# A pre-norm attention and channel-mix block on one Trainium2 core: pair sums of the last group moved to VectorE, and four seams between the stages rearranged

## The chip, the core and the metric

The kernel runs on one core of one Trainium2 chip. Its time is that of the whole program on the device, in microseconds, as a median over runs. Five engines work side by side, each through its own queue of instructions, in order: TensorE (PE, with its weight loads as PEld), VectorE (DVE), ScalarE (ACT), GpSimd (POOL) and SyncE (SP), which only issues transfers here. They meet through semaphores.

## What is computed

Cut to what matters, for `x` of shape (8, 1024, 512) in fp32:

```
x = x + attn(layernorm(x));   x = x + mix(layernorm(x))

attn(x): ct_q = x Wdq + b;  q = heads(ct_q Wuq + b) + heads(rope(ct_q Wqr + b))
         ct_kv = x Wdkv + b; k = heads(ct_kv Wuk + b) + heads(rope(x Wkr + b)); v = heads(ct_kv Wuv + b)
         softmax(q k^T / scale) v  (16 heads of 32)  -> Wo + b
mix(x):  x_prev = x shifted by one token
         xr = mu_r x + (1 - mu_r) x_prev;  xk = mu_k x + (1 - mu_k) x_prev
         sigmoid(xr Wr^T) * (relu(xk Wk^T)^2 Wv^T)
```

## The kernel before

All products are taken with operands split into a high part in the format of TensorE's fast fp32 and a low remainder, as high*high + high*low + low*high, so each product has three matmuls for each 128 of depth. Work goes through four stages, each a block that ends when all engines have ended it: `fold_block` (weights multiplied together), `project_block`, `attend_block`, `mix_block`.

**Projection.** 16 chunks of 512 tokens (two per batch). In each, eight items give q and k, four give v; the high and low parts go through a ring of four buffers to memory. In the last chunk TensorE also computes, between the items, the score products of which the row maxima of the first attention group are taken (`max_product`, with VectorE's `max_reduce`); these maxima are needed before the exponentials.

**Attention.** 32 groups, each of four heads of one batch, in three slots (`load_group` brings q, k and v of a group by ten loads on SP's queue). A group has two halves of queries; a half has four units, a unit eight score products `scores` of 128 keys x 512 queries (L977). ScalarE takes each to its exponential (L1097), `pv` multiplies them with the values (L990), and GpSimd adds the two halves of a unit's exponentials pairwise (L1124), joins the four pair sums to two (one by an accumulating transfer, L1128, and one by an addition, L1131), whose column sums TensorE takes in `sums` (L1004). ScalarE may be three units ahead of pair sums and values. Between its scores TensorE computes the maxima products of the next group (L413), in the order `USE`: 32 tiles of half 0, two of half 1, the transpose of half 0's row maxima (L408), 30 tiles, the transpose of half 1. VectorE reduces each (L429) and writes the negated maxima (L426); SP copies them under the q stack (`stack_max`). How many maxima stand before each score is the table `SPREAD`: one before each of the eight, a second one at the third score of unit 4 (this is where the transpose of half 0 comes to lie), and one behind the value unit of unit 7. The first group has a table of its own, since its next group is loaded only at the start of this stage: none in its first two units, eleven in each of the others. Slot 1 lies in memory that only this stage owns; slots 0 and 2 are overlaid with buffers of other stages.

In the last group there are no more maxima. Meanwhile VectorE inverts the softmax sums of seven batches (L1148), multiplies the heads of the mix's first chunk with them (L1151), and takes the low parts of two weights and of that chunk. ScalarE makes their high parts (L1071, L1094), between units. GpSimd adds the pairs of all units but the last.

**Mix.** 16 chunks again. TensorE's order in chunk c is: output projection of chunk c+1 (`project`), key product (out of `xk`), receptance product (`xr`), transposes of the normalised chunk c+1, value product; 48 matmuls each but for the transposes. The others' work runs a chunk ahead. VectorE: residual of chunk c+1 (L1509; TensorE's key product waits for it tile by tile, since it reuses its banks), statistics, normalise (L1525), four low parts of the squared relu (L1594, `square_lo`), the shift (difference L1537, mix L1540 and L1548, with the four gatings L1603 between), and low parts of it (L1583, L1585). GpSimd: power for the deviation, four squares (L1469), the product of the heads of chunk c+2 with the inverse sums (L1442, `divide`), their low part (L1446, `o_low`), the final additions and bias additions in turn (L1482, L1451). ScalarE: relu, high parts, sigmoid. The prologue of this stage prepares chunks 0 and 1; the shift of its chunk 0 is done by quarters of the features (`first_shift`), all others whole.

## Time and profile before

| | |
|---|---|
| median of 3 runs | 3108.95 us (3105.3 to 3110.42) |
| profiled execution, its own time | 3107.7 us |
| its span | 3105.7 us |
| mean granted TensorE clock | 0.987 |
| TensorE busy | 3013.7 us, 97% of the span |
| VectorE, ScalarE, GpSimd busy | 2249.6 us, 1487.7 us, 2095.4 us |
| attention, from its first score product | from 661.54 us |
| mix, from its first transfer | from 2309.01 us |

Spans are measured from the first instruction; the profiled execution's own time has some 2 us around it. Busy times of TensorE are modelled, so a full slice isn't yet TensorE at its peak. The idle time of an engine that is not the bound costs nothing.

### The profile page before, as it was taken

To read this page: it belongs to the slowest core of one execution; us is meant where nothing else is said; L and a number is where in the kernel's file an instruction comes from. 1 tells how busy PE (TensorE), PEld (TensorE's weight loads), DVE (VectorE), ACT (ScalarE), POOL (GpSimd) and SP (SyncE) were. 2 spreads that over 40 slices of the span, in tenths; PEclk is the share of its full clock that TensorE was granted. 3 is DMA by queue.
4 is the path that set the end of the run, shared out by engine and by line. 5 is a ranking of instruction groups with operands and counts; after the bars stand their busy time and mean duration, and the time that the engine had idled before them with its cause. 6 is when DMAs were issued, how large, how long until landed. Compare 5 with 4: busy or idle time off the path is not lost. (4 is left out here: it accounts for less than half of the span.)

```text
span 3105.7 us, 42723 instructions
## 1 busy us (share of the span) xinstructions
PE 3013.7 (97%) x15424; PEld 2007.0 (65%) x15424; DVE 2249.6 (72%) x3352; ACT 1487.7 (48%) x2715; POOL 2095.4 (67%) x715
## 2 busy tenths in 40 slices
PE   8999999989999999999999999999987999999998
PEld 5888888855555555555555555555536787878776
DVE  5555665568777777777777777777748777777784
ACT  2222222126666666666666666666652323223222
POOL 1111121128999999999999999999974665665663
PEclk9999999989999999999999999999988999999999
DMA  4554545664646464656555565646351323323311
GB/s 147 173 173 166 177 163 174 184 158 105 138 109 147 100 147 104 146 110 137 120 127 128 121 134 122 136 111 146 86 144 41 109 74 88 108 61 101 108 54 41
DMA packets 189193, 381.77 MB, mean 123 GB/s; under 512 B 17360, under 2 KB 53360, under 8 KB 180976
## 3 DMA queue, kind: packets, MB, share of 16 engines
q1 hardware_dynamic: 179968, 313.70, 36.8%
q0 software_dynamic: 9072, 66.06, 10.4%
q8 instruction: 92, 1.51, 0.2%
q14 instruction: 61, 0.50, 0.1%
HBM read 194.59 MB, written 118.49 MB: 101 GB/s over the span
## 5 line engine op out<-in xcount | busy, mean ns | idle before, releaser
L429 DVE TENSOR_REDUCE part_max<-ps_m 128x1 f32<-128x512 f32 x1984 | 1214.4, 682 | 333.6 <-PE ps_m L413 332.8
L1124 POOL TENSOR_TENSOR pairs<-probs 128x2048 f32<-128x2048 f32 x255 | 1187.3, 4662 | 144.8 <-ACT probs L1097 133.7
L1097 ACT ACTIVATE probs<-ps_s 128x512 f32<-128x512 f32 x2048 | 1037.0, 623 | 290.9 <-PE ps_s L977 275.1
L413 PE MATMUL ps_m<-k_stack,q_stack 96*128 96x512 f32 x1984 | 820.8, 415 | 15.7 <-DVE neg_max L426 8.5
L977 PE MATMUL ps_s<-q_stack,k_stack 97*128 97x512 f32 x2048 | 818.0, 403 | 6.9 <-PEq L461 3.7
L413 PEld LDWEIGHTS ps_m<-k_stack,q_stack 96*128 96x128 f32 x1984 | 376.6, 190 | 286.9 <-DVE part_max L429 136.8
L990 PE MATMUL ps_o<-probs,v_tiles 128*32 128x512 f32 x4096 | 498.4, 605 | 0.0
L977 PEld LDWEIGHTS ps_s<-q_stack,k_stack 97*128 97x128 f32 x2048 | 389.4, 191 | 135.7 <-ACT probs L1097 21.5
L676 POOL TENSOR_TENSOR ln_rstd<-ln_rstd,ln_minus_half 128x4 f32<-128x4 f32 x15 | 15.1, 1008 | 413.5 <-DVE ln_rstd L718 413.5
L1131 POOL TENSOR_TENSOR pairs<-pairs 128x2048 f32<-128x2048 f32 x63 | 288.6, 4581 | 4.9
L990 PEld LDWEIGHTS ps_o<-probs,v_tiles 128*32 128x32 f32 x4096 | 107.6, 109 | 235.5 <-issue 177.2
L1482 POOL TENSOR_TENSOR gate<-gate,xs 128x512 f32<-128x512 f32 x64 | 115.3, 1804 | 131.7 <-DVE diff L1548 114.3
L1403 ACT ACTIVATE relu<-mix_p 128x512 f32<-128x512 f32 x64 | 38.3, 598 | 239.8 <-PE mix_p L1288 188.4
L1594 DVE TENSOR_TENSOR ka_lo<-relu,ka_hi 128x512 fp32r<-128x512 f32 x64 | 109.3, 1707 | 50.4 <-ACT ka_hi L1397 48.2
L1067 ACT COPY l_sb<-ps_s 128x512 f32<-128x512 f32 x64 | 37.5, 586 | 175.7 <-PE ps_s L1004 174.6
L1004 PE MATMUL ps_s<-pairs,ones 128*32 128x512 f32 x1008 | 119.7, 592 | 0.0
L1286 PE MATMUL mix_p<-xk_hi,mix_w_k_hi 128*128 128x512 f32 x256 | 103.7, 405 | 13.1 <-DVE xs L1509 9.0
L1451 POOL TENSOR_TENSOR xs<-mix_x_in,bo 128x512 f32<-128x512 f32 x64 | 113.2, 1773 | 4.5
L761 DVE TENSOR_TENSOR st_v<-ps_p,bv 128x512 f32<-128x512 f32 x64 | 44.2, 691 | 99.3 <-PE ps_p L595 99.3
L1469 POOL TENSOR_TENSOR relu<-relu 128x512 f32<-128x512 f32 x64 | 68.8, 1084 | 66.7 <-ACT relu L1403 66.7
L1286 PE MATMUL mix_p<-mix_w_v_hi,ka_hi 128*128 128x512 f32 x256 | 102.6, 401 | 11.3 <-DVE ka_lo L1594 11.3
L563 PE MATMUL ps_p<-xT_hi,w_q_hi 128*128 128x512 f32 x256 | 102.1, 399 | 1.5 <-DVE y_rot L783 1.5
(196 smaller groups left out, 4804.7 us busy)
## 6 DMA issues: line engine op xcount, KB each, us to landing
pairs<-pairs POOLq DMA_DIRECT2D x63, 1024.0 KB, 8.0
q_stack<-q_hi_scratch SPq DMA_DIRECT2D x128, 256.0 KB, 6.2
k_stack<-k_hi_scratch SPq DMA_DIRECT2D x64, 512.0 KB, 10.9
x_in<-in_x SPq DMA_DIRECT2D x16, 1024.0 KB, 5.6
q_hi_scratch<-st_hi SPq DMA_DIRECT2D x64, 256.0 KB, 2.2
q_lo_scratch<-st_lo SPq DMA_DIRECT2D x64, 256.0 KB, 2.5
k_hi_scratch<-st_hi SPq DMA_DIRECT2D x64, 256.0 KB, 2.4
k_lo_scratch<-st_lo SPq DMA_DIRECT2D x64, 256.0 KB, 2.6
```

Of the source, the lines that this page charges most:

```text
L413: nc.tensor.matmul(bank[:, :], att["q"][r][0:ROWS, half, h, q * P:(q + 1) * P], att["k"][r][0:ROWS, h, kc * CH:(kc + 1) * CH], start=True, ...
L429: nc.vector.reduce_max(part_max[:, half, j, kc:kc + 1], bank[:, :], AX).then_inc(att["m_read"], 1)
L977: nc.tensor.matmul(ps_s[v % SR][:, :], ks[r][:, a, kt * P:(kt + 1) * P], qs[r][:, qc, a, :], start=True, stop=True).then_inc(scored, 1)
L990: m = nc.tensor.matmul(ps_o[a * HD:(a + 1) * HD, :], vt[r][:, kt, a * HD:(a + 1) * HD], probs[:, (r * UNITS + u) % PR, k, a, :], start=kt ...
L1004: m = nc.tensor.matmul(ps_s[v % SR][a * HD:(a + 1) * HD, :], ones[:, :], pairs[:, w, a, :], start=k == 0, stop=k == SUMS - 1)
L1097: nc.scalar.activation(probs[:, (r * UNITS + u) % PR, x // HG, x % HG, :], ps_s[place(u * UT + x) % SR][:, :], ACT.Exp, scale=SCALE).then_ ...
L1124: nc.gpsimd.tensor_tensor(pairs[:, w, :, :], probs[:, (r * UNITS + u) % PR, 0, :, :], probs[:, (r * UNITS + u) % PR, 1, :, :], ALU.add).th ...
L1131: nc.gpsimd.tensor_tensor(pairs[:, 3, :, :], pairs[:, 2, :, :], pairs[:, 3, :, :], ALU.add).then_inc(pair_done, 1)
L1286: nc.tensor.matmul(out, stat_hi(f), mov_hi(f), start=f == 0, stop=False)
L1451: nc.gpsimd.tensor_tensor(xs[par][:, s, :], x_in[:, s, :], bo[:, :], ALU.add).then_inc(xb_done, 1)
L1482: nc.gpsimd.tensor_tensor(gate[s], gate[s], xs[par][:, s, :], ALU.add).then_inc(out_done, 1)
L1594: nc.vector.tensor_tensor(ka_lo[:, g, :], relu[:, g % RELU, :], ka_hi[:, g, :], ALU.subtract).then_inc(kal_done, 1)
```

## The change

1. `USE` puts the transpose of half 0 behind eight tiles of half 1 instead of two, and `SPREAD` sets it behind the value unit of unit 4.
2. The load of group 1 moves from the start of the attention into SP's queue ahead of the stores of the last projection chunk. Its slot now lies over the room of the projection's `x_in`, on the right side of the memory. SP's waits for the stacked maxima (dropped) and for the value stores (moved into the attention stage) no longer stand at the projection's end. The first group uses `SPREAD` like all others.
3. In the last group GpSimd does nothing. VectorE adds seven pairs and both joins, and makes the three high parts that were ScalarE's; the first join is an addition instead of a transfer.
4. In the mix prologue VectorE takes residual and statistics of chunk 0 first, then the product of heads of chunk 1 (GpSimd's before), the normalise, the low part of those heads (GpSimd's before), a weight, the shift by quarters, the residual of chunk 1, and only then the inverse of the last batch's sums and the low part of `xr`.
5. In every `divide` of the mix loop GpSimd first waits for the four low parts of the squared relu.
6. The shift for the last chunk is done by quarters too, and its four output tiles are stored one by one.

```diff
-USE = tiles(0, 0, HALF_TILES) + tiles(1, 0, 1) + [(0, HALF_TILES, 0)] + tiles(1, 1, HALF_TILES) + [(1, HALF_TILES, 0)]
+UNIT_TILES = HALF_TILES // 4
+USE = (tiles(0, 0, HALF_TILES) + tiles(1, 0, UNIT_TILES) + [(0, HALF_TILES, 0)]
+       + tiles(1, UNIT_TILES, HALF_TILES) + [(1, HALF_TILES, 0)])
...
+                    if last and par == CPB - 1:
+                        sp.wait_ge(transposed, B * CPB * FC)
+                        load_group(sp, att, grouped, 1, 1)
...
-            for half in range(2):
-                sp.wait_ge(att["m_stacked"][half], 16)
...
-            load_group(sp, att, scratch, 1, 1)
+            for s in att["v_stored"]:
+                sp.wait_ge(s, 16 * B * CPB)
...
-        SPREAD[ROUNDS][2] = 2
+        SPREAD[ROUNDS][UT] = 1
         SPREAD[UNITS - 1][UT] = 1
-        SPREAD_FIRST = [[0] * (UT + 1) if u < 2 else [2, 1, 1, 2, 1, 1, 2, 1, 0] for u in range(UNITS)]
...
+                pair(0)
+                pair(1)
+                pair_onto(1, n * NQ, joined_last)
+                pair(2)
+                dve.wait_ge(mix["inv_stored"], 16)
+                weight_high("o")
+                pair(3)
+                pair_onto(3, n * NQ, pair_done)
+                weight_low("o", 1)
+                pair(4)
+                weight_high("k")
                 dve.wait_ge(mix["o_loaded"], 16)
                 dve.wait_ge(mix["inv_loaded"], 16 * HG)
                 nc.vector.tensor_tensor(mix["o_in"][:], mix["o_in"][:], mix["o_lo"].bitcast(F32), ALU.mult).then_inc(mix["o_div"], 1)
-                weight_low("o", 1)
+                pair(5)
                 weight_low("k", 2)
+                dve.wait_ge(mix["o_div"], 1)
+                nc.vector.tensor_copy(mix["o_hi"], mix["o_in"][:]).then_inc(mix["oh_done"], 1)
+                pair(6)
...
                     if two_more:
+                        pool.wait_ge(kal_done, c * FC + FC)
                         divide(c + 2)
...
             weights_low(2)
+            residual(0, 0)
+            statistics(0, 0)
+            dve.wait_ge(o_loaded, 32)
+            dve.wait_ge(inv_loaded, 32 * HG)
+            nc.vector.tensor_tensor(o_in[:], o_in[:], first_inverse[:].bitcast(F32), ALU.mult).then_inc(o_div, 1)
+            normalise(0, 0)
+            dve.wait_ge(oh_done, 2)
+            nc.vector.tensor_tensor(o_lo[:], o_in[:], o_hi[:], ALU.subtract).then_inc(ol_done, 1)
+            weights_low(3)
+            dve.wait_ge(small_loaded, 16 * 3)
+            quarter_shift(0, 0, 0)
+            residual(1, 1)
             dve.wait_ge(l_loaded, 32)
             nc.vector.reciprocal(inv, sums).then_inc(inv_done, 1)
-            dve.wait_ge(small_loaded, 16 * 3)
-            norm(0, 0)
-            weights_low(3)
-            first_shift()
-            first_shift_low()
+            shift_low_r(0)
...
-                    if more:
+                    if last and par == CPB - 2:
+                        quarter_shift(c + 1, 1 - par, FC - 1, gated_value)
+                        shift_low_r(c + 1)
+                    elif more:
                         shift(c + 1, 1 - par, i if par == 0 else i + 1, gated_value)
...
+                    if last and par == CPB - 1:
+                        for s in range(TPC):
+                            sp.wait_ge(out_done, c * TPC + s + 1)
+                            sp.dma_start(out_v[i, par, :, s, :], gate[s]).then_inc(out_stored, 16)
+                        return
```

`pair(u)` is the addition of L1124 on VectorE with the same waits, `pair_onto(w, ...)` the join of two pair sums. `quarter_shift` is the former `first_shift`, with the chunk's gatings between its quarters.

## Rows read from the trace of the kernel before

**Rows 1.** Busy time by engine, steady attention: PE, PEld, DVE, ACT, POOL, clock, DMA.
```profile
760.00:2196.00 1436.00, 1428.28 (x8230) 790.16 (x8230) 1132.25 (x1929) 982.84 (x1929) 1350.15 (x342) 1.00 0.56 125
```

**Rows 2.** Timeline of VectorE, second and last transpose of half 1 (start, us, instruction).
```profile
727.54 0.28 DVE L426 TENSOR_SCALAR neg_max<-ps_m 16x128 fp32r<-16x128 f32 x1 [0.45 <-PE ps_m L408]
...
2246.52 0.28 DVE L426 TENSOR_SCALAR neg_max<-ps_m 16x128 fp32r<-16x128 f32 x1 [0.45 <-PE ps_m L408]
```

**Rows 3.** Timeline of VectorE and GpSimd, mix; eleven chunk distances between the first and last difference.
```profile
2529.03 2.29 DVE L1537 TENSOR_TENSOR diff<-xT 128x2048 f32<-128x2048 f32 x1
...
2570.01 1.96 DVE L1594 TENSOR_TENSOR ka_lo<-relu,ka_hi 128x512 fp32r<-128x512 f32 x2 [1.23 <-ACT ka_hi L1397]
2572.47 4.61 POOL L1442 TENSOR_TENSOR o_in<-o_in,o_lo 128x2048 f32<-128x2048 f32 x1 [1.88 <-DMA o_lo<-inv_scratch]
2576.31 2.91 DVE L1537 TENSOR_TENSOR diff<-xT 128x2048 f32<-128x2048 f32 x1 [4.34 <-ACT xT L1368]
...
3048.52 2.29 DVE L1537 TENSOR_TENSOR diff<-xT 128x2048 f32<-128x2048 f32 x1 [4.35 <-ACT xT L1368]
```

**Rows 4.** Timeline of TensorE, start of the attention.
```profile
661.54 8.17 PE L977 MATMUL ps_s<-q_stack,k_stack 97*128 97x512 f32 x16 [3.72 <-PEq L461]
...
679.60 0.77 PE L413 MATMUL ps_m<-k_stack,q_stack 96*128 96x512 f32 x1 [6.72 <-DMA k_stack<-k_lo_scratch]
```

**Rows 5.** Timeline of ScalarE, last group.
```profile
2266.44 1.90 ACT L1071 CAST mix_w_o_hi<-raw_o 128x2048 fp32r<-128x2048 f32 x1 [2.73 <-DMA inv_scratch<-early_inverse]
...
2275.97 4.03 ACT L1097 ACTIVATE probs<-ps_s 128x512 f32<-128x512 f32 x8 [1.92 <-PE ps_s L977]
...
2281.49 4.03 ACT L1097 ACTIVATE probs<-ps_s 128x512 f32<-128x512 f32 x8
```

**Rows 6.** Timeline of VectorE and TensorE, last group.
```profile
2277.26 6.50 DVE L1151 TENSOR_TENSOR o_in<-o_in,o_lo 128x2048 f32<-128x2048 f32 x1 [24.80 <-DMA o_lo<-inv_scratch]
...
2305.14 1.89 PE L1019 MATMUL ps_s<-probs,ones 128*32 128x512 f32 x16
```

**Rows 7.** Timeline of VectorE and TensorE, mix prologue.
```profile
2324.41 0.95 DVE L1614 RECIPROCAL gate<-gate 128x128 f32<-128x128 f32 x1 [10.47 <-DMA gate<-l_scratch]
...
2331.95 6.09 DVE L1525 TENSOR_SCALAR mixed<-xs,mix_mv,mix_rstd 128x512 f32<-128x512 f32 x4 [1.15 <-POOL mix_rstd L1435]
...
2338.10 3.58 PE L1309 MATMUL mix_t<-ident,mixed 128*128 128x128 f32 x16 [17.76 <-DVE mixed L1525]
...
2357.41 2.29 DVE L1579 TENSOR_TENSOR xr_lo<-diff,xr_hi 128x2048 fp32r<-128x2048 f32 x1 [1.96 <-ACT xr_hi L1376]
...
2360.45 0.76 PE L1286 MATMUL mix_p<-xk_hi,mix_w_k_hi 128*128 128x512 f32 x1 [7.84 <-DVE xs L1509]
```

**Rows 8.** Timeline of TensorE, first key product of the last chunk.
```profile
3062.89 0.80 PE L1286 MATMUL mix_p<-xk_hi,mix_w_k_hi 128*128 128x512 f32 x1 [4.03 <-DVE xk_lo L1583]
```

**Rows 9.** Timeline of TensorE, starts of units in one steady group, and a value unit.
```profile
1511.84 0.50 PE L413 MATMUL ps_m<-k_stack,q_stack 96*128 96x512 f32 x1
...
1518.29 0.50 PE L413 MATMUL ps_m<-k_stack,q_stack 96*128 96x512 f32 x1
...
1522.22 1.92 PE L990 MATMUL ps_o<-probs,v_tiles 128*32 128x512 f32 x16
...
1537.41 0.28 PE L408 MATMUL ps_m<-ident,row_max 128*16 128x128 f32 x1
...
1543.39 0.50 PE L413 MATMUL ps_m<-k_stack,q_stack 96*128 96x512 f32 x1
```

**Rows 10.** Groups by line: the normalise (count, total us, mean ns).
```profile
L1525 DVE TENSOR_SCALAR mixed<-xs,mix_mv,mix_rstd 128x512 f32<-128x512 f32 x64 | 55.7, 929 | 18.1 <-POOL mix_rstd L1435 18.1
```

**Rows 11.** Busy time by engine in the last group; PEclk is the seventh number.
```profile
2272.00:2276.00 4.00, 4.00 (x18) 1.17 (x11) 0.00 (x0) 2.08 (x3) 3.59 (x1) 0.50 0.97 201
```

**Rows 12.** Waits: us in total, times, longest us.
```profile
PE mix_p L1286 <- DVE ka_lo L1594: 11.3, 11, 1.5
```

**Rows 13.** Transfers: count, KB each, median us to landing.
```profile
out<-gate SPq DMA_DIRECT2D x16, 256.0 KB, 3.8
```

More of the change, by code:

```diff
@@ L497, in project_block @@
         stored = [sem(f"stored{i}") for i in range(RING)]
-        v_stored = [sem(f"v_stored{i}") for i in range(TPC)]
+        v_stored = att["v_stored"]
         block = ctx.enter_context(nc.Block())
@@ L1067, in take_l @@
                 nc.scalar.copy(l_sb[:, qc, :], ps_s[v % SR][:, :]).then_inc(exped, 1)
-            def weight_high(k):
-                act.wait_ge(mix["w_loaded"][k], 16)
-                nc.scalar.copy(mix["w_hi"][k], mix["w_raw"][k]).then_inc(mix["w_split_hi"], 1)
             def step(i, r, n):
@@ L1125, in step @@
                                             ALU.add).then_inc(pair_done, 1)
-                    if w == 1 and not at_the_end:
+                    if w == 1:
                         pool.wait_ge(pair_done, h * ADDS + 2)
@@ L1141, in weight_low, with pair, pair_onto @@
                     nc.vector.tensor_tensor(mix["w_lo"][k], mix["w_raw"][k], mix["w_hi"][k], ALU.subtract).then_inc(mix["w_split_lo"], 1)
+                def pair(u):
+                    qc, w = divmod(u, ROUNDS)
+                    h = n * NQ + qc
+                    if w == 0 and qc == 0:
+                        dve.wait_ge(joined, 16 * h)
+                        dve.wait_ge(pair_done, h * ADDS)
+                    elif w == 0:
+                        dve.wait_ge(joined_last, 1)
+                    elif w == 1:
+                        dve.wait_ge(sum_done, (h - 1) * SUMS + 1)
+                    elif w == 3:
+                        dve.wait_ge(sum_done, h * SUMS)
+                    dve.wait_ge(exped, taken(n, place(u * UT + UT - 1)))
+                    nc.vector.tensor_tensor(pairs[:, w, :, :], probs[:, (r * UNITS + u) % PR, 0, :, :], probs[:, (r * UNITS + u) % PR, 1, :, :],
+                                            ALU.add).then_inc(pair_done, 1)
+                def pair_onto(w, h, done):
+                    dve.wait_ge(pair_done, h * ADDS + w + 1)
+                    nc.vector.tensor_tensor(pairs[:, w, :, :], pairs[:, w - 1, :, :], pairs[:, w, :, :], ALU.add).then_inc(done, 1)
                 if not is_last(n):
@@ L1488, in _ @@
                 add_bias(0, 0, s)
-            divide(1)
             inv_std(0)
-            o_low(1)
             edge(0)
@@ L1527, in norm @@
                 v.then_inc(normed, 1)
+            def norm(c, par):
+                if not (type(c) is int and c == 1):
+                    residual(c, par)
+                statistics(c, par)
+                normalise(c, par)
             def shift(c, par, batch, free_bank=lambda s: None):
@@ L1645, in block_program, with overlaid @@
         t = {"ident": lasting("ident", [P, P])}
-        def overlaid(buffers, *which):
+        def overlaid(buffers, *which, side="left"):
             with ExitStack() as passing:
-                return buffers(lambda name, shape, dt=F32: passing.enter_context(nc.sbuf_tensor(name, shape, dt)), *which)
+                return buffers(lambda name, shape, dt=F32: passing.enter_context(nc.sbuf_tensor(name, shape, dt, side=side)), *which)
         slot0 = overlaid(slot_buffers, 0)
@@ L1663, in block_program @@
             "loaded": [sem(f"stack_loaded{r}") for r in range(R3)],
+            "v_stored": [sem(f"v_stored{i}") for i in range(TPC)],
             "v_loaded": [sem(f"vt_loaded{r}") for r in range(R3)],
@@ L1683, in block_program @@
                  for k in ("q_hi", "q_lo", "k_hi", "k_lo", "v_hi", "v_lo", "rot")}
-            x_in = [sb(f"x_in{i}", [P, TPC, D]) for i in range(CPB)]
+            x_in = [early.enter_context(nc.sbuf_tensor(f"x_in{i}", [P, TPC, D], F32, side="right")) for i in range(CPB)]
+            early.enter_context(nc.sbuf_tensor("slot1_rest", [P, SLOT - CPB * TPC * D], F32, side="right"))
             x_loaded = [sem(f"x_loaded{i}") for i in range(CPB)]
```

112 lines of the change are left out of this document (61 added, 51 removed).

## The prediction

> **What bounds the kernel now.** I read the page first (shares, slices, chain), then windows by stage, then the timeline of each engine around each edit. In the attention stage TensorE is the bound: over 1436 us it is busy 1428.28 us at full clock, GpSimd 1350.15, VectorE 1132.25 [rows 1]. So there only TensorE's own stretches count, as long as GpSimd, at 94%, keeps its small slack. Group to group takes (2246.52 - 727.54) / 30 = 50.63 us [rows 2]. In the mix TensorE is nearly the bound, but a ring through VectorE and GpSimd comes out slightly longer than its work: the difference of one chunk follows that of the chunk before after (3048.52 - 2529.03) / 11 = 47.23 us [rows 3]. At the seams TensorE stands still: before the first group and inside it [rows 4], behind late exponentials in the last group [rows 5, 6], 17.76 and 7.84 us in the mix prologue [rows 7], and 4.03 us before the last chunk [rows 8]. The change touches all of these.
>
> **T behind a value unit (30 groups).** Unit 4 now holds the transpose of half 0 in its middle and lasts 1518.29 - 1511.84 = 6.45 us. The transpose of half 1 is already behind a value unit, with the same queue after it, and that unit of eight scores, eight maxima and one value unit lasts 1543.39 - 1537.41 = 5.98 us, transpose included [rows 9]. The new place of half 0 is the same situation, with the same bank two tiles on and its row maxima long done. So 0.47 us a group, 30 groups: **-14.1**. Bounds: -9, if one third of it is lost to GpSimd, whose slack of (1436 - 1350) / 1436 x 50.63 = 3.0 us a group is well over 0.47; -15.5 if nothing at all is left of a wait. The stacking of half 0's maxima starts some 5 us later and is needed twenty us on; hidden.
>
> **Group 1 loaded early; the first group like the others.** Before, TensorE starts the attention at 661.54 after 3.72 us, runs two units without maxima, waits 6.72 us for the k stack of group 1, and reaches the transpose of half 1 at about 727.5: 66.0 us [rows 2, 4]. After, the ten loads of group 1 stand in the last projection chunk, and SP waits neither for the maxima's row nor for the value stores before the block ends. The first group is then a steady one, 50.63 - 0.47, less a value unit and a pair of sums that a first group hasn't (16 records, 1.92 us in the row, about 1.8 each) = 46.5 us. TensorE has stood still before it and its clock is then at 1.2 GHz: the matmul at 679.60 takes 0.77 us where one behind a value unit took 0.50 [rows 4, 9]; I add 3 us for that, as much as some 15 matmuls at 0.43 instead of 0.23. 66.0 - 49.5 = -16.5, and about -1.2 for SP's shorter wait: **-17.7**. Bounds: -21 without the clock's loss, -11 if twice that and the loads' cost come. The loads: SP issues them ahead of all stores of the last projection chunk, where it otherwise waits for the first low half, and its queue is shared by both. VectorE sets the pace of that chunk and gets its input from a ring of four, so a store may be late by three items without harm. If the cover were gone, the whole transfer would show, which the 6.72 us of [rows 4] size; it is the lower bound above. The copies of the row of ones and the load of group 2 follow as before, with half the traffic beside them.
>
> **Last group.** Its eight pair sums, each 4.6 us on GpSimd, and both joins go to VectorE, the DMA join becomes an addition, and ScalarE loses three copies. Price on VectorE: 128x2048 with two SBUF inputs took 2.29 us with GpSimd idle [rows 3]; 7 pairs + 2 joins + 4 mix operations = 13 x 2.3, three copies of 2.3 each (no row shows a VectorE copy; it lies between nothing and 4 x 0.93 = 3.7, what four normalises of together as many elements took [rows 10]; I take 2.3, the two-input price, as the nearest in shape), and the reciprocal, about 5: 42 us in a group of over 50, and 46 at the upper price. VectorE therefore keeps up, unless it waits: its product of heads waits for the inverse, which landed at 2277.26 [rows 6], and pair 5, weight k and everything behind it are queued there; pair 4 is ahead of it and its exponentials end near then, so nothing waits. The gain is what ScalarE waited: it stood 2.73 us for the stored inverse and copied 1.90 us, then 1.89 us for weight k, where the plain distance of units is 2281.49 - 2275.97 = 5.52 us [rows 5]. Laid out anew: 0.4 + 8 x 5.52 + 2 sums of 1.8 + 2.8 (three pair sums) + 1.8 + 1.8 = 54.6 us after 2246.52, that is 2301.1, against 2305.14 + 1.89 = 2307.03 [rows 6]: -5.9. But TensorE's clock was at 1.2 GHz from 2272 to 2276 [rows 11], after units in which ScalarE's pace left it waiting; that will recur in part. **-5**, bounds -8 and 0.
>
> **Mix prologue.** Before, VectorE idles 10.47 us for the last group's sums, in the queue behind a weight and four inverses, and only then takes the residuals, though TensorE had finished them at 2338.10 - 17.76 = 2320.34. From 2324.41 to the normalise at 2331.95 are 7.54 us, of which 0.95 the reciprocal and 2.4 four residuals; 4.2 stay. New: 2320.34 + 0.7 + 4.2 + 2.3 (product of heads, now VectorE's) = 2327.5, and four normalises not held by GpSimd's o_low: 4 x 0.93 = 3.7 at most instead of 6.09 [rows 7, 10]; transposes at 2331 instead of 2338.10. From there to the first key product, 2360.45, were 22.4 us. Added o_low 2.3; gone from that path are the wait of 1.96 and the 2.29 of xr_low, since the residual of chunk 1 stands ahead of them: 20.4. 2351.1 against 2360.45: **-9.3**. GpSimd's bias additions still fall on the quarter shift, as before. What is put off: the last inverse is stored some 5 us into the first key product, so ScalarE's first relu is about 1 us late and SP's loads for chunk 2 are behind it; the product that needs these has over 10 us. Bounds -12 and -5.
>
> **GpSimd's product waits for all four ka_low (14 chunks).** This is the place where a rule and the wish part. Before, the product is issued ahead of the last ka_low, which then takes until its end, and TensorE waits 11.3 / 11 = 1.0 us for it [rows 12]. Twice the inverse was late, so that the trace shows what the edit will do every time: the two last ka_low took 1.96 us together, the product started 1.88 us late and ended at 2577.08, and now the next difference met it and took 2.91 instead of 2.29 us [rows 3]. From difference to last ka_low in that chunk: 2571.97 - 2529.03 = 42.94 us; plus 0.1 and 4.6 for the product, less 0.15 (2.91 - 2.29 against 0.77 of overlap): the ring is 47.4 to 47.5 us, against 47.23. So the wait moves from TensorE's value product to its key product, behind a residual: **+2.6** for 13 distances. Bounds: -9, TensorE's own 46.5 us; +5, if 0.15 isn't given back and an inverse is late.
> The Trainium skill, page "SBUF — State Buffer", section "Who interferes with whom", says that a VectorE operation with two SBUF inputs and a GpSimd one that reads SBUF exclude each other for a whole instruction, whoever comes first. By that rule the collision is only handed on, as the row has it (the sum +2.6); without it the sum would be the -9 above.
>
> **Last chunk by quarters, and its stores.** TensorE waits 4.03 us for xk_low and goes on at 1.2 GHz: its first matmul takes 0.80 us where one after a short wait took 0.50 [rows 8, 9]; about twelve at 0.43 for 0.23 lose 2.4. By quarters VectorE can start with the first transposed quarter, some 1.4 us ahead of the 3048.52 of [rows 3], and needs four differences, four mixes and four lows of 0.6 to 0.8 us each and three gates between, 15 x 0.68 = 10.2 us: xk_low is done at about 3057.3, ahead of the value product's end at 3062.89 - 4.03 = 3058.9: **-6.4**, bounds -7.5 and -3. The last store is 256 KB alone; behind 768 KB it took 3.8 us to land [rows 13], of which its own share by size is a quarter and a fixed part isn't known: **-1.3**, between 0 and -2.8.
>
> **Sum.** -14.1 - 17.7 - 5 - 9.3 + 2.6 - 6.4 - 1.3 = -51.2, from the profiled execution's own 3107.7 us (span 3105.7): 3056.5. That execution lies 1.25 us under the median 3108.95; so **3057** as a median.
>
> **Rivals.**
> A: the ring is not what holds the mix, and the wait on ka_low frees TensorE: 46.5 us a chunk instead of 47.4. Sum -9 in place of +2.6: 3046. For it: TensorE waited for ka_lo at 11 places, 11.3 us in all [rows 12]. Against it: the two late products [rows 3].
> B: the moved transpose gives nothing, because GpSimd at 94% or the banks take it back: -37, 3071. Against it: the twin at half 1 [rows 9].
> C: the early load disturbs the last projection chunk, or the first group runs long at 1.2 GHz: about 12 us less, 3069. For it: the slow start of [rows 4, 11].
> D, slower than before: the later product makes o_low late. Product, ScalarE's copy and o_low are a line; if o_low then lost the port to the whole shift, it would end some 9 us after TensorE wants to project, 14 times 9 = 126 us: 3057 + 126 = 3183. Counted from the end of the transposes, the product ends at 1.9, copy and o_low take 1.9 + 4.6 and up to 0.4 behind the difference, 8.8; the value product's 48 matmuls last 11. So the slack is 2.2 us, and the sum turns round from 2.2 + 51 / 14 = 5.8 us of lateness. Against it: the product comes only 1 us later, and in the late chunks the ring hardly grew [rows 3].
>
> **Chances and range.** Forecast 0.65, A 0.13, B 0.08, C 0.10, D 0.04. The forecast's own range, its bounds combined as independent, is 3047 to 3067; A and C stretch it: **3043 to 3071**. What can be told from no change here is 0.2%, 6 us. Faster 0.95, same 0.01, slower 0.04.
>
> **What will show it.** Transposes of half 0 followed by no wait, groups of 50.2 us. No long wait for k_stack, the first group under 52 us. No GpSimd work in the last group, and its units 5.5 us apart. First key product about 41 us after the first projection. ka_low never above 1.2 us, but differences of 2.9 us and waits of key products for the residual; a chunk of 47.4 us. No wait before the last key product. I am wrong if a group is still 50.6, if the mix's chunk is under 47, or if the exponentials of the last group wait for VectorE's pairs.

## The result and the profile after

The changed kernel takes 3060.54 us as a median of four runs, against 3108.43 of the kernel before beside it: a ratio of 0.9848, 95% interval 0.9831 to 0.9865. The forecast was 3057, range 3043 to 3071. The profiled execution took 3059.14 us itself, its span is 3057.4 (before 3107.7 and 3105.7), so the traces differ by 48.3 us of span. One execution of a kernel below (the product by quarters with spread matmuls) took 14671.14 us and is left out of its median. The rows that answer to those of before follow, stage by stage.

Timeline of VectorE: the transposes of half 1 that answer to [rows 2]; between them lie 30 groups.
```profile
708.94 0.28 DVE L429 TENSOR_SCALAR neg_max<-ps_m 16x128 fp32r<-16x128 f32 x1 [0.49 <-PE ps_m L411]
...
2215.86 0.28 DVE L429 TENSOR_SCALAR neg_max<-ps_m 16x128 fp32r<-16x128 f32 x1 [0.49 <-PE ps_m L411]
```
The first came 18.6 us earlier, and the group is (2215.86 - 708.94) / 30 = 50.23 us, 0.40 less.

Timeline of TensorE: the start of the attention ([rows 4]) and, in a later group, unit 4 with the transpose of half 0 ahead of it, and the sums behind it ([rows 9]).
```profile
660.10 0.77 PE L416 MATMUL ps_m<-k_stack,q_stack 96*128 96x512 f32 x1 [2.03 <-PEq L464]
...
1487.17 0.50 PE L416 MATMUL ps_m<-k_stack,q_stack 96*128 96x512 f32 x1
...
1491.12 1.92 PE L991 MATMUL ps_o<-probs,v_tiles 128*32 128x512 f32 x16
1492.98 0.28 PE L411 MATMUL ps_m<-ident,row_max 128*16 128x128 f32 x1
1493.01 0.48 PE L416 MATMUL ps_m<-k_stack,q_stack 96*128 96x512 f32 x1
1493.63 0.50 PE L416 MATMUL ps_m<-k_stack,q_stack 96*128 96x512 f32 x1
...
1498.85 1.90 PE L1007 MATMUL ps_s<-pairs,ones 128*32 128x512 f32 x16
```
The maxima start in the first unit, and the wait of 6.72 us for the k stack is gone; from the first matmul to the transpose of half 1 are 48.8 us instead of 66.0. The plain unit lasts 1492.98 - 1487.17 = 5.81 us, the next one, transpose included, 1498.85 - 1492.98 = 5.87.

Timeline of TensorE in the last group, and two 4 us stretches of it by engine (PEclk is the seventh number), for [rows 6, 11].
```profile
2219.25 1.92 PE L991 MATMUL ps_o<-probs,v_tiles 128*32 128x512 f32 x16
...
2224.96 3.35 PE L991 MATMUL ps_o<-probs,v_tiles 128*32 128x512 f32 x16
...
2244.64 3.39 PE L991 MATMUL ps_o<-probs,v_tiles 128*32 128x512 f32 x16
...
2251.80 3.58 PE L991 MATMUL ps_o<-probs,v_tiles 128*32 128x512 f32 x16
...
2272.23 1.90 PE L1022 MATMUL ps_s<-probs,ones 128*32 128x512 f32 x16
```
```profile
2224.00:2228.00 4.00, 4.00 (x18) 1.01 (x22) 2.29 (x1) 1.75 (x4) 0.00 (x0) 0.57 1.04 399
2244.00:2248.00 4.00, 4.00 (x19) 0.81 (x18) 4.00 (x3) 1.64 (x4) 0.00 (x0) 0.62 0.00 0
```
Three of the group's eight value units (from 2224.96 on) run at half clock, between 1.92 us ones. GpSimd is idle, as meant, and TensorE ends at 2274.13, 58.3 us after the transpose of half 1; before it was 60.5.

Timeline of TensorE in the prologue: first projection, transposes, first key product, for [rows 7].
```profile
2276.31 0.47 PE L1318 MATMUL mix_p<-mix_w_o_hi,o_hi 128*128 128x512 f32 x1 [2.18 <-PEq L854]
2296.45 3.46 PE L1341 MATMUL mix_t<-ident,mixed 128*128 128x128 f32 x16 [9.01 <-DVE mixed L1568]
2316.58 0.77 PE L1318 MATMUL mix_p<-xk_hi,mix_w_k_hi 128*128 128x512 f32 x1 [5.73 <-DVE xs L1546]
```
The 17.76 us of waiting are 9.01, the 7.84 are 5.73; from first projection to first key product 40.27 us, before 2360.45 - 2309.21 = 51.24.

Timelines of VectorE and GpSimd in the mix, for [rows 3]: the first difference, one chunk, and the fourteenth difference.
```profile
2343.26 2.29 DVE L1586 TENSOR_TENSOR diff<-xT 128x2048 f32<-128x2048 f32 x1 [8.28 <-ACT xT L1400]
...
2574.41 1.96 DVE L1651 TENSOR_TENSOR ka_lo<-relu,ka_hi 128x512 fp32r<-128x512 f32 x2 [1.23 <-ACT ka_hi L1433]
2580.01 3.35 DVE L1586 TENSOR_TENSOR diff<-xT 128x2048 f32<-128x2048 f32 x1 [3.64 <-ACT xT L1400]
...
2961.44 3.38 DVE L1586 TENSOR_TENSOR diff<-xT 128x2048 f32<-128x2048 f32 x1 [3.60 <-ACT xT L1400]
```
```profile
2576.61 4.60 POOL L1480 TENSOR_TENSOR o_in<-o_in,o_lo 128x2048 f32<-128x2048 f32 x1 [1.62 <-DVE ka_lo L1651]
```
The waits of TensorE, in total us, times, longest, for [rows 12]:
```profile
PE mix_p L1318 <- DVE xs L1546: 21.3, 14, 5.7
```
The ka_low are undisturbed. The product starts 0.24 us behind the last of them and ends at 2581.21, 1.20 us after the difference was issued, which therefore takes 3.35 instead of 2.29. TensorE's wait for ka_low has become one for the residual ahead of the key product. Thirteen distances are 618.18 us. Before, the same two differences stood at 2387.79 and 3001.24, 613.45 us apart: this stage costs 4.7 us. One of the thirteen is 48.37 us long: there the inverse landed late, and the product stood 0.91 us behind the last ka_low. Some 0.8 of the 4.7 is that.

In the last chunk there is no wait for xk_low. Timeline of SyncE's queue and GpSimd: the last two stores, which one row holds, and GpSimd's last addition:
```profile
3052.13 3.10 SPq L1304 DMA_DIRECT2D out<-gate  x2
3053.62 1.26 POOL L1521 TENSOR_TENSOR gate<-gate,xs 128x512 f32<-128x512 f32 x1 [1.51 <-DVE gate L1660]
```

| term | forecast | trace |
|---|---|---|
| T behind a value unit, 30 groups | -14.1 | -12.1 |
| early load, first group | -17.7 | -18.6 |
| last group, to the first projection | -5 | -2.2 |
| prologue (forecast to the first key product, trace to the first difference of the loop) | -9.3 | -11.6 |
| product waits for ka_low, 13 distances | +2.6 | +4.7 |
| last chunk, 14th difference to last gate product | -6.4 | -6.6 |
| stores | -1.3 | -1.9 |
| sum | -51.2 | -48.3 |

### The profile page after: what moved, and what is told of

Same layout as the page of the kernel before. It is cut to its first block and busy times, and to the rows that moved or that the text cites. A ratio compares the mean times of both kernels' runs of the same rounds, so it can differ in the third digit from the quotient of the medians.

```text
span 3057.4 us, 42730 instructions
## 1 busy us (share of the span) xinstructions
PE 2998.4 (98%) x15424; PEld 2002.8 (66%) x15424; DVE 2216.4 (72%) x3372; ACT 1480.5 (48%) x2715; POOL 2041.7 (67%) x704
## 5 line engine op out<-in xcount | busy, mean ns | idle before, releaser
L1113 POOL TENSOR_TENSOR pairs<-probs 128x2048 f32<-128x2048 f32 x248 | 1155.6, 4672 | 110.2 <-ACT probs L1087 110.1
L1546 DVE TENSOR_TENSOR xs<-mix_p,xs 128x512 f32<-128x512 f32 x64 | 43.8, 688 | 85.7 <-POOL xs L1489 81.2
L1318 PE MATMUL mix_p<-mix_w_o_hi,o_hi 128*128 128x512 f32 x256 | 100.1, 391 | 2.4 <-PEq L854 2.2
```

The lines of the kernel that those rows point to most:

```text
L1113: nc.gpsimd.tensor_tensor(pairs[:, w, :, :], probs[:, (r * UNITS + u) % PR, 0, :, :], probs[:, (r * UNITS + u) % PR, 1, :, :], ALU.add).th ...
L1318: nc.tensor.matmul(out, stat_hi(f), mov_hi(f), start=f == 0, stop=False)
```

## The experiments

Every time is a median beside runs of the kernel before on the same chip; the intervals of the ratios are 0.0013 to 0.0017 to either side, 4 to 5 us. So sizes below that are read from the stages of the traces, each of one execution. "The changed kernel" is the one of the diff.

### The wait on ka_low: taken away, and loosened by one

```diff
-                        pool.wait_ge(kal_done, c * FC + FC)
                         divide(c + 2)
```


> The changed kernel, but GpSimd's product of heads no longer waits for the four ka_low. Theory (the wait only hands the collision on, and costs a little): the mix's distance from difference to difference falls from 47.65 us back to about 47.2, the differences (3.3 us in the changed kernel) take 2.3 again, the last ka_low reach past 2 us, and TensorE waits about 1 us a chunk for ka_low instead of for the residual; 13 x 0.43 = 5.6 us less than the changed kernel's 3060.5: about 3055. Rival A of the prediction (the wait frees TensorE): without it the distance grows, 3070 or more.

Measured: 3052.66 us, ratio 0.9825 (0.9811 to 0.9838). Thirteen distances are 613.74 us, 47.21 each; the difference is 2.29 (2.93 once, behind a late inverse), TensorE waits 11.2 us for ka_low in 12 places. Timelines of one chunk, VectorE and GpSimd:
```profile
2667.28 6.14 DVE L1650 TENSOR_TENSOR ka_lo<-relu,ka_hi 128x512 fp32r<-128x512 f32 x2 [1.23 <-ACT ka_hi L1433]
2673.76 2.29 DVE L1585 TENSOR_TENSOR diff<-xT 128x2048 f32<-128x2048 f32 x1 [0.34 <-ACT xT L1400]
```
```profile
2667.82 5.05 POOL L1480 TENSOR_TENSOR o_in<-o_in,o_lo 128x2048 f32<-128x2048 f32 x1
```
All as before the change: the product goes first, and the last ka_low gets its turn when it ends. Rival A falls (without the wait the distance would have grown). The sign of the term is shown: in five other kernels with the same wait and product (T in its old place, the old list, the late load, the lump, the whole last chunk) the thirteen distances are 617.2 to 617.8 us (620.2 and 621.4 in two more, with late inverses), against 613.45 and 613.74 without the wait.

```diff
-                        pool.wait_ge(kal_done, c * FC + FC)
+                        pool.wait_ge(kal_done, c * FC + FC - 1)
```


> The changed kernel, but the product of heads waits for three of the four ka_low. In the changed kernel it starts 1.62 us after the last ka_low ends, and one ka_low lasts 0.98 us; with this wait it should start some 0.6 us after the last, collide with neither it nor, for more than 0.1 us, the next difference (2.3 to 2.4 us instead of 3.3). Theory of the lock between a two-input VectorE operation and GpSimd's: the distance is 46.6 to 46.9 us, 13 x 0.9 = 12 us less than the changed kernel's 3060.5, about 3049. Rival: the product lands in the last ka_low as without a wait, distance 47.2, 3055. Second rival: TensorE's own work is the floor, and no wait helps: 3060.

Measured: 3056.57 us, 0.9836 (0.9823 to 0.985); thirteen distances 614.09 us, 47.24 each. The theory, 46.6 to 46.9 us and 3049, fell; the distance is the first rival's. Timelines of one chunk, VectorE and GpSimd:
```profile
2528.57 1.96 DVE L1651 TENSOR_TENSOR ka_lo<-relu,ka_hi 128x512 fp32r<-128x512 f32 x2 [1.23 <-ACT ka_hi L1433]
2534.26 2.88 DVE L1586 TENSOR_TENSOR diff<-xT 128x2048 f32<-128x2048 f32 x1 [3.72 <-ACT xT L1400]
```
```profile
2529.95 5.04 POOL L1480 TENSOR_TENSOR o_in<-o_in,o_lo 128x2048 f32<-128x2048 f32 x1 [0.79 <-DVE ka_lo L1651]
```
I had read the 1.62 us ahead of the product as the time from ka_low to it. They are GpSimd's idle time; the product had stood 0.24 us behind the last ka_low all along. Issued earlier it is now the one that is held (5.04 us instead of 4.60), and ends at 2534.99, still 0.7 us into the difference. Between the last ka_low and the difference are 3.6 to 3.7 us, and the product needs 4.6: in that stretch no place of the wait makes it fit.

### The product in four instructions

```diff
-                nc.gpsimd.tensor_tensor(o_in[:], o_in[:], o_lo[:].bitcast(F32), ALU.mult).then_inc(o_div, 1)
+                for f in range(FC):
+                    v = nc.gpsimd.tensor_tensor(o_in[:, f, :], o_in[:, f, :], o_lo[:, f, :].bitcast(F32), ALU.mult)
+                v.then_inc(o_div, 1)
...
-                        pool.wait_ge(kal_done, c * FC + FC)
                         divide(c + 2)
```


> The changed kernel without the wait on ka_low, and GpSimd's product of heads cut into four instructions of 128x512. Without the wait in one piece the product goes first and the last ka_low ends some 4 us late (3052.7 as a median). Theory (VectorE and GpSimd exclude each other for a whole instruction, so VectorE's last ka_low gets its turn behind one quarter of 1.15 us instead of behind 4.6): TensorE's waits for ka_low are gone, the product ends 0.7 to 1 us later than in one piece, the next difference loses at most one quarter, and the distance from difference to difference falls from 47.22 to between 46.5 us, TensorE's own work, and 46.8: 13 x 0.55 = 7 us less than 3052.7: 3046. Rival 1 (GpSimd keeps the SBUF between instructions that stand in a row): the last ka_low is as late as in one piece, 47.2, 3053. Rival 2 (every hand-over costs, or the late quarters push ScalarE's copy and o_low back): 47.5 and more, 3057.

Measured: 3054.42 us, 0.9831 (0.9819 to 0.9844); thirteen distances 616.23 us, 47.40 each. Timelines of one chunk, VectorE and GpSimd:
```profile
2618.40 2.94 DVE L1652 TENSOR_TENSOR ka_lo<-relu,ka_hi 128x512 fp32r<-128x512 f32 x2 [1.23 <-ACT ka_hi L1433]
2624.02 3.09 DVE L1587 TENSOR_TENSOR diff<-xT 128x2048 f32<-128x2048 f32 x1 [2.69 <-ACT xT L1400]
```
```profile
2619.49 5.47 POOL L1481 TENSOR_TENSOR o_in<-o_in,o_lo 128x512 f32<-128x512 f32 x4 [0.52 <-DMA o_lo<-inv_scratch]
```
The mechanism is as the theory has it: the ka_low gets its turn behind a quarter, 2.94 us for the two instead of 6.14, and TensorE waits for it no more. But the four now last until 2624.96, the difference loses 0.8 us, and the theory's 46.5 to 46.8 us fell. TensorE waits for the residual instead (8.7 us in 11 places) and for o_low (2.9 us in three). One distance is 49.93 us: GpSimd stood idle for 2.92 us until the inverse landed, and TensorE's projection then waited 2.11 us for o_low. The last seven are 47.25 in the mean, against 47.21 in one piece without the wait. So the quarters gain nothing rather than lose; rival 2 was right in kind.

### T in its old place

```diff
-UNIT_TILES = HALF_TILES // 4
-USE = (tiles(0, 0, HALF_TILES) + tiles(1, 0, UNIT_TILES) + [(0, HALF_TILES, 0)]
-       + tiles(1, UNIT_TILES, HALF_TILES) + [(1, HALF_TILES, 0)])
+USE = tiles(0, 0, HALF_TILES) + tiles(1, 0, 1) + [(0, HALF_TILES, 0)] + tiles(1, 1, HALF_TILES) + [(1, HALF_TILES, 0)]
...
-        SPREAD[ROUNDS][UT] = 1
+        SPREAD[ROUNDS][2] = 2
```


> The changed kernel, but the transpose of half 0 stands where it stood before, in the middle of unit 4 (two tiles ahead of the second score). Theory (it costs what its unit lasts longer): a group takes 50.63 us instead of 50.23, 30 x 0.40 = 12 us more than 3060.5: 3072.5. Rival B (GpSimd at 94% or the banks set the group): a group stays at 50.2 and the time within 2 us of 3060.5.

Measured: 3073.38 us, 0.9897 (0.9881 to 0.9912). Timeline of VectorE, first and last transpose of half 1 over 30 groups:
```profile
709.89 0.28 DVE L427 TENSOR_SCALAR neg_max<-ps_m 16x128 fp32r<-16x128 f32 x1 [0.48 <-PE ps_m L409]
...
2230.92 0.28 DVE L427 TENSOR_SCALAR neg_max<-ps_m 16x128 fp32r<-16x128 f32 x1 [0.48 <-PE ps_m L409]
```
A group takes 50.70 us, 0.47 more than with the new place. Rival B falls.

### The early load, and the list of the first group

Old list alone, the load stays early:
```diff
+        SPREAD_FIRST = [[0] * (UT + 1) if u < 2 else [2, 1, 1, 2, 1, 1, 2, 1, 0] for u in range(UNITS)]
...
+                spread = SPREAD_FIRST if is_first(n) else SPREAD
```


> The changed kernel with the early load of group 1, but with the first group's old list of maxima: none in the first two units and ten or eleven in each later one. It parts the 18.6 us by which the first neg_max of group 1 came earlier. Theory (two halves: the wait of 6.72 us for the k stack goes with the load, the rest with the even list): the last neg_max of group 1 stands 66.0 - 6.7 = 59.3 us after the first score, that is at about 719.5 instead of 708.94, and the time is 10.5 us more than 3060.5: 3071. Rival (the early load is the whole gain, and the list only moves work within the group): within 3 us of 3060.5.

Measured: 3070.09 us, 0.9884 (0.9869 to 0.99); the transpose of half 1 at 719.59, no wait for the k stack. So the load gives some 8 us and the list some 10.6. That the list needs the load follows from the code, its first maxima read group 1; no run has the new list without it. Part of the 10.6 is the clock: from the first score to this transpose it is 0.88 of full with the old list, 0.95 in the changed kernel from its first matmul on.

The load back at the start of the attention as well, and SP's wait for the value stores back at the end of the projection (the dropped waits for the maxima stay out):
```diff
-                    if last and par == CPB - 1:
-                        sp.wait_ge(transposed, B * CPB * FC)
-                        load_group(sp, att, grouped, 1, 1)
...
+            for s in v_stored:
+                sp.wait_ge(s, 16 * B * CPB)
...
-            for s in att["v_stored"]:
-                sp.wait_ge(s, 16 * B * CPB)
+            load_group(sp, att, scratch, 1, 1)
```


> The changed kernel with the load of group 1 back at the start of the attention stage, the value stores waited for ahead of it, and the old list of the first group: this part of the change undone as a whole. Theory: the last neg_max of group 1 is back at 727.5, the k stack is waited for some 6.7 us, and the time is 18.6 us more than 3060.5: 3079. Rival (part of the gain is taken back later, by GpSimd's slack or by the loads of group 2): 3065 to 3074.

Measured: 3078.96 us, 0.9911 (0.9895 to 0.9926); the transpose at 728.09, a wait of 7.38 us for the k stack. 18.4 us more than the changed kernel, nothing of it taken back: the experiment's rival falls, and rival C of the prediction with it.

### The last group: added matmuls, in a lump and spread

```diff
+                def fill(n, r):
+                    pe.wait_ge(m_read, (n + 1) * USES)
+                    for k in range(4):
+                        nc.tensor.matmul(ps_m[k][:, :], ks[r][:, 0, k * P:(k + 1) * P], qs[r][:, 0, 0, :], start=True, stop=True)
...
                     if u >= 1:
+                        if is_last(n):
+                            fill(n, r)
                         pv(n, i, r, u - 1)
```


> The changed kernel with four more matmuls of 128x512, whose result nobody reads, ahead of each of the last group's seven value units inside the unit loop: 0.92 us of work of TensorE's in each 5.5 us in which it waits for the exponentials. Theory (the last group is longer than the sum had it because the granted clock falls to 1.2 GHz in three stretches, where a value unit takes 3.35 to 3.58 us instead of 1.92 and the next exponentials start 1.5 to 3.4 us late): the granted clock stays at 2.4 GHz, the exponentials start 5.5 to 5.9 us apart, and TensorE ends the group 3 to 5 us earlier: 3057. Rival (the value units of the last group are long because their data come late, or because VectorE's pairs hold them): clock and length stay, or the fillers lengthen the group by up to 7 x 0.92 = 6.4 us: 3060 to 3067.

Measured: 3065.03 us, 0.9864 (0.9849 to 0.9879). The distance from the last neg_max to the first projection is 70.2 us instead of 60.45. Stretches of the group, by engine, the clock the seventh number:
```profile
2220.00:2224.00 4.00, 4.00 (x18) 0.78 (x17) 3.13 (x1) 1.60 (x4) 3.92 (x2) 0.57 0.00 0
2228.00:2232.00 4.00, 4.00 (x17) 1.53 (x19) 0.00 (x0) 0.77 (x2) 0.00 (x0) 0.50 1.07 391
2260.00:2264.00 4.00, 4.00 (x22) 0.86 (x24) 0.00 (x0) 0.00 (x0) 0.00 (x0) 0.50 0.00 0
```
Over that distance the granted clock is 0.88, against 0.92 without them, and where it is at half the lump takes 1.91 us for four. But the lump lengthens the units that run at full clock too:
```profile
2240.10 1.92 PE L991 MATMUL ps_o<-probs,v_tiles 128*32 128x512 f32 x16
...
2246.55 1.92 PE L991 MATMUL ps_o<-probs,v_tiles 128*32 128x512 f32 x16
```
They stand 6.45 us apart, in the changed kernel 5.51 (2239.14 and 2244.64). Seven times 0.94 is 6.6 of the 9.7 us, about what the rival had; by this estimate the clock is the rest. TensorE's waits lie between the scores and not ahead of the value unit, so the lump filled none. The theory as I had put it, that any work in the wait will do, fell.

One matmul behind each of scores 3 to 7, where a steady group has its maxima:
```diff
+                if is_last(n):
+                    pe.wait_ge(m_read, (n + 1) * USES)
...
                         maxima(SPREAD[u][x])
+                        if is_last(n) and x >= 3:
+                            nc.tensor.matmul(ps_m[x % MR][:, :], qs[r][0:ROWS, 0, 0, 0:P], ks[r][0:ROWS, 0, 0:CH], start=True, stop=True)
```


> The changed kernel with one more matmul of 128x512, whose result nobody reads, behind the maxima's place of each of scores 3 to 7 in each unit of the last group, as a steady group has one maximum there, and none in a lump. In the first run with added matmuls the lump of four stood ahead of the value unit, while the five scores before it still went at one per exponential (2.5 us for five), and the clock fell all the same. Theory 2 (what must be filled are those five gaps of 0.3 us, and the clock then stays at 2.4 GHz as in the steady groups): the granted clock is above 0.95 in each 4 us of the last group, a value unit 1.92 us, and from the last neg_max to the first projection of the mix 56 to 58 us instead of 60.45: time 3057 to 3059. Rival (the last group's half clock doesn't depend on such gaps): two to five stretches at half clock remain, each added matmul costs 0.2 to 0.45 us, the same distance is 60 to 72 us, and the time 3060 to 3072.

Measured: 3058.75 us, 0.9847 (0.9834 to 0.9861). The matmul stands ahead of the score in the code. The group by engine, and the first product of the prologue behind it:
```profile
2216.00:2268.00 52.00, 51.56 (x316) 21.70 (x316) 36.94 (x17) 34.02 (x68) 6.37 (x2) 1.00 0.35 106
...
2272.00:2276.00 4.00, 4.00 (x13) 3.11 (x13) 3.58 (x2) 0.15 (x1) 4.00 (x2) 0.64 1.03 349
```
The clock stays at 2.4 GHz through the group, each value unit takes 1.92 us (the last, at the end, 1.90), and the distance is 56.11 us. More matmuls were added than in the lump (40 against 28), and the clock held. But the median gained little: the clock falls in the prologue's first product instead, which makes it 21.76 us from first projection to transposes against 20.14, and in this execution an inverse landed late in two chunks (the differences took 5.41 and 4.10 us).

The traces of the other kernels settle the size. In eight of them the last group's code is that of the changed kernel, and the distance is 57.2, 57.3, 58.9, 60.4, 60.5, 60.5, 60.5 and 62.2 us, 59.7 in the mean. The distance follows the number of value units at half clock: one at 57.2 and 57.3, two at 58.9, three at 60.4 and all three 60.5, four at 62.2. In the three kernels with spread matmuls there is none, and it is 56.1 each time. So half clock costs the changed last group 1.1 to 6.1 us by execution, 3.6 in the mean, and where the spread matmuls save this, 1.6 is lost again in the prologue.

The kernel before had three such units too. Timeline of TensorE, its last group:
```profile
2262.72 3.47 PE L990 MATMUL ps_o<-probs,v_tiles 128*32 128x512 f32 x16
...
2271.56 3.64 PE L990 MATMUL ps_o<-probs,v_tiles 128*32 128x512 f32 x16
...
2297.76 3.25 PE L990 MATMUL ps_o<-probs,v_tiles 128*32 128x512 f32 x16
```

### The last group as it was

```diff
-                if is_last(n):
-                    return
...
+                    if is_last(n) and u == ROUNDS - 1:
+                        act.wait_ge(mix["inv_stored"], 16)
+                        weight_high("o")
```
with the pair sums and joins of the last group on GpSimd and the three copies on ScalarE, all as in the lines that the diff removes.

> The changed kernel with the last group as it was: pair sums on GpSimd, join by DMA, and three copies on ScalarE. Theory (of the forecast 5 us this part gave 2.3 by the traces, because half clock ate the rest): from the last neg_max to the first projection 62.7 us instead of 60.45, and the prologue also loses up to 2, since o_low and weight k come later: 3063. Rival (the part is worth its forecast 5 or more, since the early order of the prologue leans on it): 3066 to 3068.

Measured: 3062.81 us, 0.9857 (0.9843 to 0.9871); 62.49 us to the first projection and 21.76 from there to the transposes, against 60.45 and 20.14. 3.7 us in the stages. The group has three value units at half clock again (3.46, 3.64 and 3.06 us), as many as the changed one, so the 2.0 us by which it is longer are not of the clock. In this execution two inverses landed late, so that the total says no more than that the part is small.

### The last chunk in one piece

```diff
-                    if last and par == CPB - 2:
-                        quarter_shift(c + 1, 1 - par, FC - 1, gated_value)
-                        shift_low_r(c + 1)
-                    elif more:
+                    if more:
```
and the same on ScalarE.

> The changed kernel, but the shift of the last chunk in one piece, as in every other chunk; the stores by quarters stay. Theory: TensorE waits about 4 us again before the last key product and goes on at 1.2 GHz, and the time is 6.9 us more than 3060.5: 3067.4. Rival (in the changed kernel, whose last product of heads isn't there to be met, part of the 6.9 us comes from the ring and not from the quarters): 3063 to 3065.

Measured: 3063.36 us, 0.9858 (0.9843 to 0.9873). Timeline of TensorE:
```profile
3022.82 0.76 PE L1318 MATMUL mix_p<-xk_hi,mix_w_k_hi 128*128 128x512 f32 x1 [4.04 <-DVE xk_lo L1637]
```
The wait is back. From the 14th difference to the last gate product are 97.34 us against 91.41: 5.9 in the trace, of which the medians, uncertain by 4 us, show 2.8. The rival would explain that number too; the trace speaks for the theory.

### The two edits that shortened a stage, together

The spread matmuls with the product by quarters, and with the product in one piece and no wait:

> The kernel with the product of heads by quarters, and with it the added matmuls of the last group, one behind each of scores 3 to 7, whose result nobody reads. In the changed kernel these cut the last group by 4.3 us, of which 1.6 were lost again in the prologue's first product at half clock. Theory: the two add up, 2.5 us less than the product by quarters alone; 3043.5. Rival (the clock's loss comes back elsewhere in the mix): no less than with the quarters alone.

Measured: 3055.26 us, 0.9831 (0.9818 to 0.9844), no less than with the quarters alone (3054.42); the rival.

> The changed kernel without the wait on ka_low, its product of heads in one piece, and the added matmuls of the last group, one behind each of scores 3 to 7, whose result nobody reads: the two edits that each made the changed kernel's traces shorter. Theory (they lie in different stages and add up): 4.3 us less in the last group, 1.6 lost again in the prologue's first product, so 2.7 us less than the 3052.7 without the wait alone: 3050, with a distance of 47.2 us in the mix. Rival (what the last group gives, the mix's first chunks take back, as beside the quarters, where the medians showed nothing): 3052 to 3055.

Measured: 3052.28 us, 0.9818 (0.9805 to 0.9831). The last group again takes 56.1 us at full clock:
```profile
2216.00:2268.00 52.00, 51.13 (x305) 22.07 (x308) 38.69 (x18) 34.16 (x68) 8.19 (x2) 1.00 0.33 106
```
It is the fastest of all kernels run, some 0.3% under the changed one, whose interval it only touches; that the matmuls add anything to the missing wait (3052.66) isn't shown, and the rival fits as well as the theory. In its trace one distance in the mix, with a late inverse, is 50.02 us. Distances of 48.4 to 50.0 us stand in six of the traces after the change, with and without added matmuls, in the changed kernel's too; what makes an inverse late was not looked into.

## Why the prediction held, point by point

**T behind a value unit.** Right, and the size between the two measures: 12.1 us from before to after, 14.1 in the traces when undone. No wait follows the transpose: the second product of maxima starts 0.62 us behind the first, in the plain unit 0.58, and the unit is 0.06 us longer than that one.

**Early load and first group.** Right: 48.8 us where the sum had 49.5, half clock at its start and nowhere else. The last projection chunk is undisturbed: the attention starts at 660.10, before at 661.54 and with the late load at 659.83, and undoing load and list costs the whole 18.4 us.

**Last group.** Right in sign, short in size: 2.2 us for 5, and the step that failed is the price of the clock. The new group was laid out at full clock, 54.6 us to its end and so some 56.8 to the first projection, and the kernels at full clock bear that out with 56.1. But it was taken from a measured group that had three value units at half clock, so their loss counted as gained, and only 0.9 us was given back for "that will recur in part". It recurred whole: three units again, 4.3 us in this execution and 1 to 6 in others. At the same number of such units the move to VectorE is worth 2.0 to 2.2 us (62.69 and 62.49 against 60.45). VectorE's pairs never held ScalarE: all its waits in this group are for TensorE. A copy of 128x2048 took 1.22 us, not the 2.3 that I chose between 0 and 3.7; it changed nothing, since VectorE had room. The Trainium skill, page "VectorE: DVE Perf Modes", section "The perf-mode tier table", has 1227 ns for it; the trace agrees.

**Prologue.** Right, 11.0 us to the first key product for 9.3: the four normalises took 1.92 us together, where 3.7 had been the price from a mean that holds longer ones (in the first chunk of the loop two took 1.27 us each and two 0.53). Added up as written, 2327.5 + 3.7 + 20.4 is 2351.6 and the forecast -8.9, not -9.3. Only this part and the stores weren't undone by an experiment; for them the trace alone speaks.

**Product behind ka_low.** Right in mechanism and sign, mis-sized: 4.7 us for 2.6, close to the upper bound of 5. The prediction's own terms, 42.94 + 0.1 + 4.6 - 0.15, are 47.49 us, and that is 3.4 over thirteen distances, not 2.6. The product stands 0.24 us behind the last ka_low where 0.1 was put, and one inverse was late. With five other kernels at 617.2 to 617.8 us, the wait alone costs some 4. The row that the terms came from had the difference 4.34 us behind the last ka_low; in the steady ring it stands 3.64 behind, and the collision is 1.1 us instead of 0.6. In four placements of the same product the distance was 47.21, 47.24, 47.40 and 47.55 us in the mean, never the 46.5 that the prediction calls TensorE's own without a row. By the trace that is about right: 47.55 less the wait for the residual, 15.6 us in 13 places, is 46.35. The page "SBUF — State Buffer" of the Trainium skill, section "Who interferes with whom", has the lock between the two engines last for a whole instruction, first come; the held ka_low, difference and product (6.14, 3.35 and 5.04 us) all agree.

**Last chunk, stores.** -6.6 and -1.9 for -6.4 and -1.3.

**The rivals.** A and B were refuted by the runs that undo their step, C by the late load. D didn't come: in a steady chunk o_low ran from 2583.37 to 2587.97, behind the difference and some 2 us ahead of the projection, as counted. By quarters and behind a late inverse that slack did run out, once by 2.11 us. For the median, 3056.5 + 1.25 is 3057.75 rather than 3057. The sum was 2.9 us too hopeful: 6.9 by the last group, the ring and the 30 groups, less 4.0 that prologue, early load and the end gave beyond theirs. That the median came within 4 us is in part luck: the last group's miss was covered by terms that gave more than forecast.

## What to carry to other kernels

Where two engines shut each other out for a whole instruction, as VectorE and GpSimd do here, moving one of the two only changed who waits; measure the free stretch between the other's instructions first, and if it is shorter than the piece, keep the order that measures shorter, here the product first. An idle stretch in front of an instruction is the engine's, not the distance from the instruction that it waited for: take that from the two timelines. A stage whose pace another engine sets can lose TensorE's clock, so price it at both levels, count the units at half clock on both sides of a comparison, and look at several executions before calling its length a number.

## What the hardware showed that I hadn't expected

The same code of the last group had one to four of its eight value units at half clock in eight traces, each of another kernel. TensorE counts as busy throughout these units. Ahead of them the last five scores had started 0.49 us apart, at the pace of the exponentials, but so they had ahead of units that stayed at full clock; what picks the unit is not shown. Four added matmuls in a lump ahead of each value unit didn't keep the clock (0.88 over the group), five spread between the scores kept 2.4 GHz in three kernels out of three (56.1 us). The prologue's first product then falls to 0.64 of the clock in one stretch of 4 us. It does so behind the lump too (0.68), and behind the old last group in the run that puts it back (0.63), but not in the trace of before, which has the same last group (1.00), nor behind the changed one in any of the eight; why stays open. The Trainium skill, page "TensorE: Matmul & The Clock Gate", Part 1, says of the first matmuls of a kernel that the same kernel has a different number at half clock from run to run. No run here shows that for the start; in the last group the eight traces show a number that varies as well.

GpSimd lets VectorE in between two of its instructions that stand in a row: of the four quarters the second, at 2620.74, took 1.73 us with the last ka_low in between, the others 1.28 or 1.29. All four took 5.47 us, instead of 4.60 in one piece; some 0.4 of that is the part of the cutting itself, since undisturbed quarters start 1.24 us apart.
